# Tokens of the first feed-forward shared out, the first attention's tail reordered, and products that nobody reads added at waits of TensorE

## The chip, the cores and the metric

The kernel runs on one core of one Trainium2 chip, as one launch. The metric is the device time of that launch in microseconds. TensorE (PE in the profile) multiplies matrices, VectorE (DVE), ScalarE (ACT) and GpSimd (POOL) do the elementwise work, and SyncE (SP) issues all DMAs. The engines run side by side and wait for each other by semaphores only.

## The reference

The input x has 8 sequences of 256 tokens with 512 features, and a context of 8 x 256 x 128. Two layers follow, each an attention onto the context and a feed-forward, all with a layernorm before and a residual after:

```
x = x + L0_xattn(layernorm(x), ctx)     # 16 heads of 32, causal, softmax(q k / sqrt(32)) v, Wout
x = x + L0_ffn(layernorm(x))            # tokens rounded to 8 bits, weights to -1, 0, 1; silu between
x = x + L1_xattn(layernorm(x), ctx)     # 16 heads with latent keys of 64 (rope on the context)
x = x + L1_ffn(layernorm(x))            # 8 experts of width 16, the 2 best of each token
```

In L0_ffn a token row is divided by its own largest magnitude over 127 and rounded, multiplied by W1 (512 x 2048), and the hidden row is treated in the same way ahead of W2 (2048 x 512).

## The kernel before, in words

Everything is in tiles of 128 tokens. There are 16 tiles, two to a sequence, and X holds them all in SBUF with their means and variances (mv) and inverse deviations (rstd). The program is a row of blocks. In a block each engine has its own instruction list, and all engines meet before the next block begins. The blocks are: layer0_attention, layer0_feed_forward, score_weights (weight products of the second attention), the second attention itself (layer1_attention) and layer1_experts.

**Split products.** Where full precision is wanted, a matrix a is kept as a_h (ScalarE writes it, rounded) and a_l = a - a_h (VectorE or GpSimd), and `products` (L41) issues three products for each pair: low by high, high by low, high by high. A projection of the first attention (`project`, L396) is 12 such products for the queries and 3 for the keys.

**The first attention.** TensorE follows a list of steps written out by hand: BEGIN0, then FIRST0 for batch 0, STEPS0 for batches 1 to 7 and END0 (L185). For every group i of four heads there are: `S` the scores, `TY`, `TZ`, `TX` the transposes of the probabilities (keys 0 for heads 0 and 1, keys 0 for heads 2 and 3, keys 1), `pv` the product with the values, and `proj` the projection of the next batch. `lnt` transposes normalised tokens, `v` makes values, and `out` is the output projection of one tile of tokens: 12 products of 512 columns. Every step but S writes one of four PSUM banks in turn, and `take_bank` (L340) lets TensorE wait until the holder of four steps ago has been read. Around a group, VectorE finds the maxima (L757), ScalarE does the exponentials (L524), VectorE inverts the sums (L766), GpSimd multiplies the probabilities (`normalise`, L667). Then ScalarE copies the transposed keys 0 and VectorE keys 1 (`copy_probs`). After pv, ScalarE and VectorE split the result (`split_c`), and the two tiles of out need the split of all four groups.

Beside that, the weights W1 and W2 are brought to -1, 0, 1 in pieces at numbered positions of each batch (`weights_at`), on VectorE as one operation of 128 x 512 a piece (`quantise`, L834). Three of the pieces fall on positions 5, 6 and 7 of the last batch.

**The first two tiles of the feed-forward** are prepared in the attention's block. GpSimd normalises them in the last batch between groups 2 and 3 (`early_tokens`, L686). VectorE rounds them (`quantise_early_tokens`, L965): a maximum, four small operations and two passes of 512, with a drain after most. Tile 0 is transposed on TensorE (`xt`) and copied by ScalarE into early_xqT. Tile 1 is transposed in the feed-forward's block.

**The feed-forward** (`step`, L1041) is a loop over t from -2 to 15. At each t, TensorE transposes the rounded hidden row of tile t, multiplies tile t + 2 by W1 (`up`, 16 products of 512 columns), multiplies tile t by W2 (`down`, 16 products) and transposes the tokens of tile t + 3.

**The start.** Tiles 0 and 1 of x and the matrix Wq are the first loads. VectorE measures both tiles (L850 to L860), GpSimd makes the inverse deviations in six small operations (`pool_deviations`, L160), VectorE normalises both tiles (L867), and TensorE transposes both once the second is done (L386). ScalarE rounds the four quarters of Wq (L581) ahead of all else, and VectorE makes the four low parts (L871). The first projection waits for both transposed tiles, split, and for all four low parts.

## Time and profile before

| | us |
|---|---|
| median of 3 runs | 1033.93 |
| lowest and highest | 1032.07 to 1035.49 |
| the profiled execution's own time | 1032.81 |
| its span, from the first to the last instruction | 1030.8 |
| outside the span | 2.0 |

The profile is of one execution. Its blocks end at about 284.4 (first attention), 422.4 (feed-forward), 444.6 (weight products) and 981 us (second attention). Times in the rows are microseconds from the span's start. An x and a number after a tile's name says how many instructions of that kind the row merges, and its duration then runs from the first start to the last end. "idle before" in square brackets is how long the engine had stood still, with what it waited for. TensorE's clock has two levels, 1.2 and 2.4 GHz, shown as 0.50 and 1.00 of the granted clock.

### The profile page before, as it was taken

What the parts mean: (1) busy time and instruction counts of PE and PEld (TensorE: products, weight loads), DVE (VectorE), ACT (ScalarE), POOL (GpSimd) and SP (SyncE); (2) the same over time, 40 slices, a digit from 0 to 9 for tenths busy, and PEclk for the clock granted to TensorE, in tenths of its full rate; (3) what the DMA queues carried; (4) which work ended last, traced back from release to release, by engine and by line L of the source; (5) the groups of instructions that cost most, each with busy time, mean ns of one, the idle gap of its engine ahead of it and who ended that gap; (6) DMA issues with size and microseconds to landing.
All of it is one profiled execution on the core that took longest, in us unless ns stands there. A gap on an engine that the chain in (4) does not pass through costs nothing. (4 is left out here: it accounts for less than half of the span.)

```text
span 1030.8 us, 20634 instructions
## 1 busy us (share of the span) xinstructions
PE 972.3 (94%) x7756; PEld 761.5 (74%) x7772; DVE 754.6 (73%) x1646; ACT 631.0 (61%) x1691; POOL 319.8 (31%) x379
## 2 busy tenths in 40 slices
PE   5889999998789999889999999999999999999997
PEld 4677778786545555447888888888888888888796
DVE  5768998886678998266667767677676776767586
ACT  4578888786478787465555545555555555555462
POOL 5766777455534430520020020200202002000461
PEclk9899999998999999999999999999999999999998
DMA  8130121000093000530000000000000000000013
GB/s 288 39 142 2 48 89 43 2 2 2 2 255 133 1 1 1 183 104 1 1 22 1 1 22 1 22 1 1 22 1 22 1 1 1 1 2 1 1 43 123
DMA packets 20131, 41.92 MB, mean 41 GB/s; under 512 B 1216, under 2 KB 4544, under 8 KB 19520
## 3 DMA queue, kind: packets, MB, share of 16 engines
q1 hardware_dynamic: 20032, 40.59, 11.7%
q8 instruction: 63, 1.03, 0.4%
q14 instruction: 36, 0.29, 0.1%
HBM read 36.39 MB, written 4.19 MB: 39 GB/s over the span
## 5 line engine op out<-in xcount | busy, mean ns | idle before, releaser
L1577 ACT ACTIVATE c_h<-c_bank_b 128x512 fp32r<-128x512 f32 x64 | 38.3, 598 | 158.2 <-PE c_bank_b L1489 158.2
L673 POOL TENSOR_TENSOR a_probs<-a_probs,a_inv 128x256 f32<-128x256 f32 (+1 forms) x128 | 109.7, 884 | 65.6 <-DVE a_inv L774 65.1
L1591 ACT ACTIVATE probs<-c_score,c_neg_max 128x256 f32<-128x256 f32 x256 | 119.0, 480 | 9.8 <-DVE c_neg_max L1671 9.7
L533 ACT ACTIVATE a_probs<-a_s,a_neg_max 128x128 f32<-128x128 f32 (+1 forms) x256 | 104.2, 436 | 28.0 <-DVE a_neg_max L762 27.9
L1661 DVE TENSOR_TENSOR c_l<-c_bank_b,c_h 128x512 fp32r<-128x512 f32 x64 | 44.2, 691 | 103.7 <-ACT c_h L1577 103.7
L45 PE MATMUL c_acc<-VO_h,c_l 128*128 128x512 f32 x256 | 101.7, 397 | 1.4 <-DVE c_l L1661 1.4
L47 PE MATMUL c_acc<-VO_h,c_h 128*128 128x512 f32 x256 | 100.7, 393 | 0.0
L1582 ACT ACTIVATE c_pT_h<-c_turn 128x512 fp32r<-128x512 f32 x128 | 69.6, 597 | 50.3 <-PE c_turn L1479 50.3
L46 PE MATMUL c_acc<-VO_l,c_h 128*128 128x512 f32 x256 | 100.0, 391 | 0.0
L1310 POOL TENSOR_TENSOR c_ctx_raw<-c_ctx_raw,c_table 128x1024 f32<-128x1024 f32 x8 | 19.0, 2378 | 226.3 <-PE c_bank_b L1489 213.4
L1666 DVE TENSOR_TENSOR c_pT_l<-c_turn,c_pT_h 128x512 fp32r<-128x512 f32 x128 | 81.9, 681 | 1.4 <-ACT c_pT_h L1582 1.4
L1671 DVE TENSOR_REDUCE c_neg_max<-c_score 128x2 f32<-128x512 f32 x128 | 81.7, 680 | 0.8
L1679 DVE TENSOR_SCALAR probs<-probs,c_inv 128x256 f32<-128x256 f32 x256 | 75.6, 358 | 5.0
L45 PE MATMUL c_bank_a<-c_yT_h,A_l 128*128 128x256 f32 x256 | 77.1, 301 | 0.0
L162 POOL TENSOR_SCALAR c_var<-g_mean_var 128x2 f32<-128x2 f32 x7 | 1.6, 225 | 228.3 <-DVEq L1692 228.3
L47 PE MATMUL c_bank_a<-c_yT_h,A_h 128*128 128x256 f32 x256 | 72.4, 283 | 0.0
L46 PE MATMUL c_bank_a<-c_yT_l,A_h 128*128 128x256 f32 x256 | 71.9, 281 | 0.0
L1479 PE MATMUL c_turn<-g_ident,probs 128*128 128x128 f32 x512 | 69.5, 279 | 0.0
L762 DVE TENSOR_REDUCE a_neg_max<-a_s 128x2 f32<-128x256 f32 (+1 forms) x128 | 63.4, 548 | 2.7 <-PE a_s L381 2.3
L1657 DVE TENSOR_TENSOR c_qk_l<-c_bank_a,c_qk_h 128x512 fp32r<-128x512 f32 x64 | 44.0, 687 | 23.6 <-ACT c_qk_h L1573 23.6
L1479 PEld LDWEIGHTS c_turn<-g_ident,probs 128*128 128x128 f32 x512 | 55.1, 140 | 7.8 <-DVE probs L1679 0.3
L1069 PE MATMUL b_down<-w,b_hqT 128*128 128x512 bf16 x255 | 57.8, 379 | 1.6 <-ACT b_hqT L1086 1.5
(278 smaller groups left out, 2859.1 us busy)
## 6 DMA issues: line engine op xcount, KB each, us to landing
w_raw<-in_w SPq DMA_DIRECT2D x8, 1024.0 KB, 5.7
wq<-in_wq SPq DMA_DIRECT2D x1, 4096.0 KB, 23.0
c_ctx_raw<-in_ctx SPq DMA_DIRECT2D x8, 512.0 KB, 3.3
wo<-in_wo SPq DMA_DIRECT2D x1, 4096.0 KB, 14.9
out<-g_x SPq DMA_DIRECT2D x16, 256.0 KB, 2.1
g_x<-in_x SPq DMA_DIRECT2D x7, 512.0 KB, 6.5
wq_raw<-in_wq SPq DMA_DIRECT2D x4, 256.0 KB, 5.5
a_ctx_raw<-in_ctxT SPq DMA_DIRECT2D x8, 128.0 KB, 2.8
```

The lines of the kernel that those rows point to most:

```text
L45: pe.matmul(out, ll, rh, start=start and n == 0, stop=False)
L46: pe.matmul(out, lh, rl, start=False, stop=False)
L47: last = pe.matmul(out, lh, rh, start=False, stop=stop and n == len(pairs) - 1)
L533: last = act.activation(probs[i % 2][:, 2 * pair + j, at], s[:, 2 * pair + j, at], ACT.Exp, bias=neg_max[:, pair, q, j:j + 1], accum_out=s ...
L673: last = pool.tensor_tensor(p, p, inv[:, pair, q, :].unsqueeze(2).broadcast_to([P, 2, (q + 1) * P]), ALU.mult)
L762: last = dve.tensor_reduce(neg_max[:, pair, q, :], s[:, 2 * pair:2 * pair + 2, q * P:(2 * q + 1) * P], AX.X, ALU.max, negate=True)
L1479: last = pe.transpose(turn[k][:, hq * P:(hq + 1) * P], probs[p % 2][:, hq, k * P:(k + 1) * P], ident[:, :])
L1582: act.activation(pT_h[:, k, :], turn[k][:, :], ACT.Copy).then_inc(turn_hi, 1)
L1591: last = act.activation(probs[p % 2][:, i, :], score[h][:, t, :], ACT.Exp, bias=neg_max[:, i:i + 1], accum_out=sums[:, i:i + 1])
L1666: dve.tensor_tensor(pT_l[:, k, :], turn[k][:, :], f32(pT_h[:, k, :]), ALU.subtract).then_inc(turn_lo, 1)
L1671: dve.tensor_reduce(neg_max[:, 2 * h:2 * h + 2], score[h][:, :, :], AX.X, ALU.max, negate=True).then_inc(maxed, 1)
L1679: last = dve.tensor_scalar(probs[p % 2][:, i, :], probs[p % 2][:, i, :], inv[:, i:i + 1], None, ALU.mult)
```

## The change: what it does

1. **Start.** VectorE clears a small tile (`blank`) and TensorE then multiplies it 36 times (128 x 128 by 128 x 256, bf16) into a bank that nobody reads. VectorE takes over the small operations of the first inverse deviations; GpSimd keeps the power alone. TensorE transposes a tile as soon as that tile is normalised. GpSimd makes two of the four low parts of Wq, ahead of its copy of the identity.
2. **Last batch of the first attention.** The three pieces of W2 at positions 5, 6 and 7 move behind the rounding of both early tiles. VectorE goes straight from the maxima of group 3 to both copies of keys 0 of group 2 (ScalarE's before), the inversion and copy that follow, and the split of group 1. GpSimd no longer normalises the early tiles; VectorE does so inside quantise_early_tokens.
3. **END0.** A step "fill0" of 5 products of 512 columns comes first. It takes a bank, as every step does. Both early tiles are transposed (xt0, xt1) between out0 and out1, and ScalarE copies both.
4. **Feed-forward.** Tile 1 comes ready from the block before, so its transpose and copy go. Products that nobody reads are added: 9 of 512 columns ahead of tile 1's up products, and in the last tile 10 of 256 columns ahead of the wait for the rounded hidden row, 4 ahead of the down products, 16 behind them.
5. **Weight products.** 10 products of 512 columns follow TensorE's last transpose of this block.

The diff, cut to its core:

```diff
+def keep_awake(pe, out, left, right, n):
+
+    for _ in range(n):
+        pe.matmul(out, left, right, start=True, stop=True)
...
-END0 = ["pv2'", "T3'", "pv3'", "xt0", "out0'", "out1'"]
+END0 = ["fill0", "pv2'", "T3'", "pv3'", "out0'", "xt0", "xt1", "out1'"]
...
-                sp.wait_ge(wq_lo, DC)
+                sp.wait_ge(wq_lo, DC // 2)
+                sp.wait_ge(wq_lo_pool, DC // 2)
+                sp.wait_ge(y_turned, 1)
...
-                        pe.wait_ge(y0_ready, 1)
+                        pe.wait_ge(y0_ready, i + 1)
...
-                            pe.wait_ge(wq_lo, DC)
+                            pe.wait_ge(wq_lo, DC // 2)
+                            pe.wait_ge(wq_lo_pool, DC // 2)
...
+                def keep_busy(n):
+
+                    for _ in range(n):
+                        pe.matmul(s[:, 0, 0:S], blank[:, 0:P], blank[:, :], start=True, stop=True)
+
+                pe.wait_ge(blanked, 1)
+                keep_busy(36)
...
+                    elif kind == "fill":
+                        keep_awake(pe, out[:, :], identb[:, :], mask[:].rearrange("p q k -> p (q k)"), 5)
                     elif kind == "xt":
-                        turn_early_tokens(out)
+                        turn_early_tokens(i, out)
...
-                copy_probs(B - 1, 2)
                 split_c(B - 1, 2)
                 copy_probs(B - 1, 3)
                 split_c(B - 1, 3)
-                act.wait_ge(early_turned, 1)
-                act.activation(early_xqT.rearrange("p c t -> p (c t)"),
-                               work[bank_of["xt", 0, 0]][:, 0:D // 2].bitcast(BF16), ACT.Copy)
+                for i in range(TPB):
+                    act.wait_ge(early_turned, i + 1)
+                    act.activation(early_xqT[:, i].rearrange("p c t -> p (c t)"),
+                                   work[bank_of["xt", 0, i]][:, 0:D // 2].bitcast(BF16), ACT.Copy)
...
-                def early_tokens():
-                    pool.wait_ge(y_turned, TILES)
-                    for i in range(TPB):
-                        pool.tensor_scalar(y[:, i, :], X[:, i, :], mv[:, i, 0:1], rstd[:, i:i + 1], ALU.subtract, ALU.mult
-                                           ).then_inc(early_y_ready, 1)
...
-                deviations(0).then_inc(rstd0_ready, 1)
-                pool.wait_ge(y0_ready, 1)
+                pool.drain()
+                pool.wait_ge(first_var_ready, 1)
+                pool.tensor_tensor(rstd[:, 0:TPB], first_var[:, :], power[:, :], ALU.pow).then_inc(first_root_ready, 1)
                 pool.wait_ge(ident_in, DMA)
+                for c in range(DC // 2, DC):
+                    pool.wait_ge(wq_hi, c + 1)
+                    pool.tensor_tensor(wq_l[:, c, :], wq_raw[:, c, :], f32(wq_h[:, c, :]), ALU.subtract).then_inc(wq_lo_pool, 1)
...
-                    if b == B - 1:
-                        early_tokens()
...
+                def copy_first_keys(b, i, pair):
+                    dve.wait_ge(p_turned, 3 * (b * 4 + i) + pair + 1)
+                    dve.tensor_copy(pT[:, 2 * pair:2 * pair + 2, 0:S],
+                                    work[bank_of["TZ" if pair else "TY", b, i]][:, :].rearrange("p (h t) -> p h t", h=2)
+                                    ).then_inc(k0_copied, 1)
...
+                dve.memset(blank[:, :], 0.0).then_inc(blanked, 1)
                 first_statistics(0)
                 first_statistics(1)
-                measure(0)
-                dve.wait_ge(rstd0_ready, 1)
+                dve.drain()
+                for tile in range(TPB):
+                    dve.bn_aggr(mv[:, tile, :], first_stats[:, tile, :])
+                dve.drain()
+                first = slice(0, TPB)
+                dve.tensor_scalar(first_var[:, :], mv[:, first, 1], EPS, None, ALU.add).then_inc(first_var_ready, 1)
+                dve.wait_ge(first_root_ready, 1)
+                dve.tensor_tensor(first_sq[:, :], rstd[:, first], rstd[:, first], ALU.mult)
+                dve.drain()
+                dve.tensor_tensor(first_sq[:, :], first_sq[:, :], first_var[:, :], ALU.mult)
+                dve.drain()
+                dve.tensor_scalar(first_sq[:, :], first_sq[:, :], -0.5 * SCALE, 1.5 * SCALE, ALU.mult, ALU.add)
+                dve.drain()
+                dve.tensor_tensor(rstd[:, first], rstd[:, first], first_sq[:, :], ALU.mult)
+                dve.drain()
                 for i in range(TPB):
-                    last = dve.tensor_scalar(y[:, i, :], X[:, i, :], mv[:, i, 0:1], rstd[:, i:i + 1], ALU.subtract, ALU.mult)
-                last.then_inc(y0_ready, 1)
-                for c in range(DC):
+                    dve.tensor_scalar(y[:, i, :], X[:, i, :], mv[:, i, 0:1], rstd[:, i:i + 1], ALU.subtract, ALU.mult
+                                      ).then_inc(y0_ready, 1)
+                for c in range(DC // 2):
                     dve.wait_ge(wq_hi, c + 1)
                     dve.tensor_tensor(wq_l[:, c, :], wq_raw[:, c, :], f32(wq_h[:, c, :]), ALU.subtract).then_inc(wq_lo, 1)
                 split_y(0, 0)
...
-                    weights_at(b, 5)
+                    if b < B - 1:
+                        weights_at(b, 5)
                     if b == 0:
                         first_statistics(6)
                         measure(5)
                     split_proj(b + 1, 2)
                     copy_probs(b, 1)
-                    weights_at(b, 6)
+                    if b < B - 1:
+                        weights_at(b, 6)
 
                     maxima(b, 3, 0)
                     maxima(b, 3, 1)
+                    if b == B - 1:
+                        copy_first_keys(b, 2, 0)
+                        copy_first_keys(b, 2, 1)
+                        invert(b, 3, 0)
+                        copy_probs(b, 2)
+                        split_c(b, 1)
+                        break
...
-                    dve.wait_ge(early_y_ready, i + 1)
+                    dve.tensor_scalar(y[:, i, :], X[:, i, :], mv[:, i, 0:1], rstd[:, one], ALU.subtract, ALU.mult)
+                    dve.drain()
...
-                copy_probs(B - 1, 2)
+                dve.wait_ge(early_rstd_ready, 1)
+                dve.wait_ge(y_turned, TILES)
                 quantise_early_tokens(0)
                 split_c(B - 1, 2)
                 copy_probs(B - 1, 3)
                 split_c(B - 1, 3)
                 quantise_early_tokens(1)
+                for pos in (5, 6, 7):
+                    weights_at(B - 1, pos)
...
+                def awake(t, n):
+                    out = down[:, :] if t < 0 else xT[:].rearrange("p c t -> p (c t)").bitcast(F32)
+                    keep_awake(pe, out, identb[:, :], w1[:, 0, 0:D if t < 0 else S], n if t < 0 else 2 * n)
+
                 def step(t, par):
+                    if t == -1:
+                        awake(t, 9)
+                    if t == TILES - 1:
+                        awake(t, 5)
...
-                        tokens = xqT if t + 2 > 0 else early_xqT
-                        if t + 2 > 0:
-                            pe.wait_ge(x_copied, t + 2)
+                        tokens = xqT if t + 2 >= EARLY else early_xqT[:, t + 2]
+                        if t + 2 >= EARLY:
+                            pe.wait_ge(x_copied, t + 3 - EARLY)
...
+                    if t == TILES - 1:
+                        awake(t, 2)
...
-                    if has(t, 3):
-                        rounded = xq[1 - par] if t + 3 >= EARLY else early_xq[t + 3]
-                        after(pe, x_quant, t + 4 - EARLY)
-                        after(pe, x_copied, t + 2)
+                    if t + 3 >= EARLY and has(t, 3):
+                        pe.wait_ge(x_quant, t + 4 - EARLY)
+                        after(pe, x_copied, t + 3 - EARLY)
                         for c in range(DC):
-                            last = pe.transpose(xT[:, c, :], rounded[:, c * P:(c + 1) * P], identb[:, :])
+                            last = pe.transpose(xT[:, c, :], xq[1 - par][:, c * P:(c + 1) * P], identb[:, :])
                         last.then_inc(x_turned, 1)
                 all_steps(pe, step)
+                awake(TILES, 8)
...
+                keep_awake(pe, banks[0][:, :], identb[:, :], identb[:, :].unsqueeze(1).broadcast_to([P, 4, P]), 10)
```

## Rows read from the trace of the kernel before

**Rows 1.** The page: busy time by engine

```profile
PE 972.3 (94%) x7756; PEld 761.5 (74%) x7772; DVE 754.6 (73%) x1646; ACT 631.0 (61%) x1691; POOL 319.8 (31%) x379
```

**Rows 2.** Stretches: length; busy PE, PEld, DVE, ACT, POOL; clock, DMA

```profile
284.40:422.40 138.00, 128.32 (x812) 67.53 (x828) 113.91 (x216) 103.87 (x96) 41.80 (x21) 1.00 0.25 73
...
422.40:444.60 22.20, 18.83 (x168) 11.23 (x168) 6.40 (x9) 12.47 (x21) 13.79 (x13) 1.00 0.72 261
...
444.60:981.00 536.40, 531.03 (x3505) 442.47 (x3505) 375.95 (x799) 284.65 (x807) 64.17 (x79) 1.00 0.03 9
...
46.70:49.50 2.80, 2.48 (x29) 2.19 (x26) 2.79 (x6) 1.05 (x3) 2.28 (x5) 0.50 0.32 56
...
244.80:254.50 9.70, 8.65 (x70) 6.05 (x67) 4.21 (x9) 5.15 (x20) 4.16 (x5) 0.50 0.01 3
```

**Rows 3.** Order of time, TensorE after two waits (start, duration, idle before)

```profile
45.13 0.66 PE L425 MATMUL a_work<-g_ident,a_probs 128*128 128x128 f32 x4 [2.23 <-DVE a_c_l L788]
...
422.52 1.71 PE L1224 MATMUL cw_bank<-kcq,wqr 128*64 128x128 f32 x27 [2.13 <-PEq L1031]
```

**Rows 4.** Order of time, VectorE, ScalarE, GpSimd in the first 15 us

```profile
7.83 1.00 DVE L867 TENSOR_SCALAR y<-g_x,g_mean_var,g_rstd 128x512 f32<-128x512 f32 x2 [2.69 <-POOLq L173]
...
7.35 2.61 ACT L581 ACTIVATE wq_h<-wq_raw 128x512 fp32r<-128x512 f32 x4 [5.35 <-DMA wq_raw<-in_wq]
...
8.91 2.49 POOL L701 CAST g_identb<-g_ident 128x128 bf16<-128x128 f32 x1 [1.16 <-DVE y L867]
...
12.98 1.54 POOL L703 TENSOR_TENSOR wkv_l<-wkv_raw,wkv_h 128x512 fp32r<-128x512 f32 x1 [1.59 <-ACT wkv_h L588]
```

**Rows 5.** Order of time, TensorE, the first projections

```profile
12.50 0.58 PE L45 MATMUL a_work<-a_yT_h,wq_l 128*128 128x256 f32 x1 [1.57 <-DVE a_yT_l L746]
...
15.81 0.28 PE L45 MATMUL a_work<-a_yT_h,wq_l 128*128 128x256 f32 x1
...
17.61 0.33 PE L376 MATMUL a_s<-a_qk_h,a_qk_l 32*128 32x128 f32 x4
```

**Rows 6.** Order of time, VectorE, last batch of the first attention

```profile
263.40 1.01 DVE L838 SCALAR_TENSOR_TENSOR w<-w_raw,a_limit,w 128x512 bf16<-128x512 f32 x1
...
264.94 0.92 DVE L838 SCALAR_TENSOR_TENSOR w<-w_raw,a_limit,w 128x512 bf16<-128x512 f32 x1
...
265.79 1.94 DVE L762 TENSOR_REDUCE a_neg_max<-a_s 128x2 f32<-128x256 f32 x4
...
277.52 0.68 DVE L968 TENSOR_REDUCE a_early_amax<-y 128x1 f32<-128x512 f32 x1
...
279.76 0.43 DVE L977 TENSOR_SCALAR early_xq<-early_yr 128x512 bf16<-128x512 f32 x1
...
283.61 0.69 DVE L802 TENSOR_TENSOR g_x<-g_x,a_work 128x512 f32<-128x512 f32 x1 [2.11 <-PE a_work L47]
```

**Rows 7.** Order of time, GpSimd and ScalarE, last batch

```profile
265.31 4.57 POOL L689 TENSOR_SCALAR y<-g_x,g_mean_var,g_rstd 128x512 f32<-128x512 f32 x2
...
269.85 3.17 POOL L673 TENSOR_TENSOR a_probs<-a_probs,a_inv 128x256 f32<-128x256 f32 x4
...
270.27 1.13 ACT L544 ACTIVATE a_pT<-a_work 128x512 f32<-128x512 f32 x2
```

**Rows 8.** Order of time, TensorE, last batch and the feed-forward's tile 1

```profile
271.55 0.96 PE L441 MATMUL a_work<-a_pT,V 128*32 128x256 f32 x8 [4.59 <-ACT a_pT L544]
...
277.75 0.47 PE L45 MATMUL a_work<-wo_h,a_c_l 128*128 128x512 f32 x1 [0.72 <-DVE a_c_l L788]
...
289.93 3.63 PE L1060 MATMUL b_up<-w,b_xqT 128*128 128x512 bf16 x16 [1.47 <-ACT b_xqT L1101]
```

**Rows 9.** Order of time, TensorE, into the second attention

```profile
444.81 0.63 PE L1445 MATMUL c_bank_a<-g_ident,c_y 128*128 128x128 f32 x4 [3.23 <-PEq L1204]
...
445.71 3.52 PE L1511 MATMUL c_acc<-wo,kckv 128*128 128x512 f32 x4
...
452.62 1.88 PE L1511 MATMUL c_acc<-wo,kckv 128*128 128x512 f32 x4
```

More of the change, by code:

```diff
@@ L199, in steps_of_layer0 @@
                 own = b + (1 if kind in ("proj", "v") or "~" in x else 0) + (2 if "+" in x else 0) - (1 if "'" in x else 0)
-                if kind == "xt":
+                if kind in ("xt", "fill"):
                     own = 0
@@ L487, in _ @@
                         add_sums(i, out)
+                    elif kind == "fill":
+                        keep_awake(pe, out[:, :], identb[:, :], mask[:].rearrange("p q k -> p (q k)"), 5)
                     elif kind == "xt":
-                        turn_early_tokens(out)
+                        turn_early_tokens(i, out)
                     else:
@@ L1098, in step @@
                                            ).then_inc(silued, 1)
-                    if has(t, 3):
-                        act.wait_ge(x_turned, t + 3)
+                    if t + 3 >= EARLY and has(t, 3):
+                        act.wait_ge(x_turned, t + 4 - EARLY)
                         act.activation(xqT[:], xT[:], ACT.Copy).then_inc(x_copied, 1)
@@ L1289, in _, with layer1_attention @@
                 dve.tensor_tensor(kr_l[:, :], kr[:, :], f32(kr_h[:, :]), ALU.subtract)
[L1292 removed]
+def layer1_attention(nc, io, X, mv, rstd, ident, identb, store, ahead, ahead_in, expert_raw, expert_in, first):
     with Memory(nc, "c") as m:
@@ L2003, in program @@
         ahead_in = g.sem("ahead_in")
-        early = ([store.place(f"early_xq{i}", 3, [P, 3, D], BF16)[:, i, :] for i in range(TPB)],
-                 store.place("early_xqT", 3, [P, 3, DC, P], BF16)[:, 2, :, :], g.sb("early_s1", [P, TPB]))
+        early = ([store.place(f"early_xq{i}", 3, [P, 4, D], BF16)[:, i, :] for i in range(TPB)],
+                 store.place("early_xqT", 3, [P, 4, DC, P], BF16)[:, 2:4], g.sb("early_s1", [P, TPB]))
         expert_raw = (g.sb("wd", [P, DC, G + E]), g.sb("wu", [P, D]), g.sb("iota", [P, E]))
```

29 lines of the change are left out of this document (17 added, 12 removed).

## The prediction, made before the changed kernel was run

> **What bounds the kernel now.** I read the page first: TensorE is busy for 94% of the span, and the next engine for 73% [rows 1]. Then the stretches. The second attention keeps TensorE busy for 531 of 536 us, so whatever comes before it moves the end one for one [rows 2]. In single stretches the granted clock is 0.50, which is the lower level of 1.2 GHz: 2.8 us at 46.7, and 9.7 us at 244.8 although TensorE was busy for 8.65 of them [rows 2]. Then the waits ahead of them, in order of time. The fall at 46.7 came 1.6 us after TensorE had stood still for 2.23 us. Another stop of 2.13 us, ahead of 422.52, was followed by no fall: the block that begins there has a clock of 1.00 [rows 2, 3]. So a stop of about 2 us may cost the clock or not. All parts of the change lie ahead of the second attention, in places where TensorE waits.
>
> **Start.** GpSimd's six small operations hold VectorE for 2.69 us ahead of the first normalised tile. ScalarE is busy with Wq from 7.35 to 9.96, and only then can it take a transposed tile [rows 4]. So the inverse deviations and the earlier transposes gain almost nothing. The first projection starts at 12.50, released by the last split tile. The split was late because VectorE first made four low parts; now it makes two, and the tiles should be split at about 11.9. But the two parts on GpSimd are a new wait. The third quarter of Wq is rounded at 9.3, and one such part costs between 1.14 and 1.54 us: 1.54 is the row of the same operation at 12.98, and 1.14 is that row less the 0.4 us in which VectorE held it. They end between 11.6 and 12.7; I take 12.1 [rows 4, 5]. What queues behind them on GpSimd is the identity copy and the values' low part, which ended at 14.5 and may now end at up to 15; both are used only from the first scores on, at 17.61 [rows 5].
>
> The row of the identity copy shows what could go wrong: 128 columns took 2.49 us, as long as VectorE's four low parts beside it [rows 4]. The Trainium skill says the same (SBUF — State Buffer, "Who interferes with whom"): a VectorE instruction with two SBUF inputs and a GpSimd instruction that reads SBUF exclude each other. By that rule GpSimd's third quarter starts only at about 9.5, when VectorE's second is done, and the trace agrees. The split of the tiles reads a bank and only one SBUF input, so by the rule it leaves GpSimd alone; if it blocked it too, the projection would start at about 13.4.
>
> The clock is the larger term. The first 15 products of the projection take 3.31 us, the next 15 take 1.80 with what follows [rows 5]: the clock was at its lower level until 15.7, which the granted clock of the profile does not show. With it up the start would gain 1.5 us. The 36 products of 256 columns run at 0.22 each from about 1.1 us: to 9.0 if all are slow, to about 7 if the clock rises on the way. Transposes follow to about 9, then TensorE waits 3 us until the projection. Stops of 2.23 us were followed by a fall, so I expect the clock to be down again for most of the projection. Bounds: 1.9 us gained (high clock, start at 12.1), 0.9 lost (start at 13.4, low clock). I take 0.3 gained, near the lower row of the clock.
>
> **Last batch.** VectorE's two pieces ahead of the maxima take 1.01 and 0.92 us, and the maxima start at 265.79 [rows 6]. Without the pieces they start at 264.0. ScalarE's exponentials follow at the same distance and end 1.8 us earlier: 268.5, where its copy starts at 270.27 now. GpSimd's early tiles (4.57 us) sit ahead of its last probabilities, which start at 269.85 and end at 273.0 [rows 7]. With the tiles gone, they wait only for VectorE's inversions at 267.3 and 268.8, and end at about 270.6.
>
> TensorE stands still for 4.59 us until ScalarE has copied keys 0 of group 2, at 271.55 [rows 8]. Now VectorE copies them: two operations of 512 columns at 0.69 [rows 6], after the maxima, so until 267.2; keys 1 until 267.9, the split of group 1 until 268.3. The fill step takes the bank of group 1's pv. It therefore waits for that split, though nobody reads its products, and pv of group 2, whose data are ready at 267.9, is queued behind it. Five products of 512 columns at 0.22 (3.63 us for 16 [rows 8]) hold it until 269.4. That is hidden: the transposes of group 3 behind it need GpSimd's 270.6. They end at 272. At the low clock the fill costs 2.2 and is no longer hidden.
>
> The next in line is VectorE. It rounds tile 0 from 268.8: 2.67 us as for tile 1 (277.52 to 280.19 [rows 6]) and 0.50 for the normalisation [rows 4], to 272.1. Then come the split of group 2, keys 1 of group 3 (0.69), pv, the split of group 3: the output projection can start at 274.6 against 277.75 [rows 8], 3.1 us earlier. Its 24 products take what they take now. Between the halves there are now two transposes instead of none, 0.3 us each, and the second needs tile 1, rounded at 274.5 + 3.2 = 277.7; the first half ends at 277.4. So the second half ends at about 280.95. The three moved pieces (3 x 0.7) and the first addition fit under it, to 280.6. The last addition ends at 281.75 where it ended at 284.30 [rows 6]: 2.55 us. Bounds: the output projection's whole 3.1, and 1.0 if the clock falls among these steps. I take 2.5.
>
> **Feed-forward.** Tile 1's up products start at 289.93, released by the copy that now goes [rows 8]. The nine products ahead of them take 9 x 0.22 = 2.0, and after tile 0's up products they end at a time that matches 290.2 of now, 0.3 later than today. ScalarE reaches tile 1's silu only at 294.1, so that is hidden. At the end TensorE waits 2.13 us for the block to close, until 422.52 [rows 3]. The 16 products (16 x 0.11 = 1.8) fit in, with little to spare: nothing to 0.1 lost. The 14 others lie in waits longer than themselves. The clock of this block is 1.00 now [rows 2], so there is nothing to win either: 0 in all, between -0.3 and 0.3.
>
> **Weight products.** TensorE stands still for 3.23 us ahead of 444.81. The next four products take 3.52 us, and four of the same shape later take 1.88 [rows 9]: the low clock again. The ten products end at about 443.7, before VectorE has closed the block, so they cost nothing, and leave a stop of 1.1 us, half of the shortest one that preceded a fall in rows 3. Three heads of two such rows each run before the projection: they take 3.9 us and would take 2.6. I take 1.3; between 0 (it falls all the same) and 1.7.
>
> **Sum.** 0.3 + 2.5 + 0 + 1.3 = 4.1 us against the profiled execution's own 1032.81, so 1028.7. That execution was 1.1 below the median of the runs, 1033.93, and for the median I say 1029.8. Three runs spread over 3.4 us, and about 0.3% (3.1 us) is what a measurement of this kernel can tell from no change.
>
> **The rivals.** (A) The clock stays up through the first projection: TensorE was at work for 8 us before the stop, where at 46.7 it had been waiting on and off. That adds 1.5: 1028.3. Against it stands the 3 us stop.
>
> (B) The clock falls in the tail. Between 268 and 274.6 TensorE has only the fill, transposes and narrow products, with gaps. In its favour: at 244.8 it was 89% busy with such work and stayed at 0.50 for 9.7 us [rows 2]. The transposes and pv of groups 2 and 3 then take 1.5 us longer and the tail gives back 1.0 instead of 2.5: 1031.3. The Trainium skill (TensorE: Matmul & The Clock Gate, Part 4) has a rule of that kind: transposes do not count as work in the same way. Rows 2 bear it out in part.
>
> (C) The added products do not hold the clock, and the change does not do what it says: only the reordering counts, 1033.93 - 2.5 = 1031.4. Against it: under the steady products of the second attention the clock reads 1.00 [rows 2].
>
> (D) Slower. If the clock is down when the output projection begins and stays down as long as at 244.8, its 24 products and tile 0's 16 up products run at twice their time. The fill costs 1.1 more and the transposes 1.5, which delays the projection by 2.6; the 24 add 5.6, the 16 add 3.5. Less the 2.5 and 1.3 won that is 8.9 slower: 1042.8. It decides from a low clock at 274.6 that lasts past 280.
>
> **How the numbers follow.** Forecast 52%, with a range of its own of 1028.3 to 1031.3; A 17%, B 18%, C 8%, D 5%. Faster by over 0.3% is a time below 1030.8: three quarters of the forecast case (0.39), nearly all of A (0.16), a quarter of B and of C (0.06), 0.61 in all. Slower by over 0.3% is D, 0.05. The rest, 0.34, is no change. The range reaches from below A to above B and C: 1026.8 to 1032.8.
>
> **What would show it.** The block after the first attention begins near 281.9 less the start's gain. TensorE's stop ahead of pv of group 2 shrinks from 4.59 to about 2. The clock row shows no 0.50 at 445, and the first four value products take 1.9. The first 15 projection products take 3.3 (forecast) or 1.7 (A). It would be wrong if GpSimd's low parts end after 13, if the fill of 5 holds back the transposes of group 3, if VectorE reaches the last addition after TensorE's last product, or if new falls of the clock appear in the first 70 us, where the shift moves every stop.

## The result: 1023.8 us where 1029.8 was forecast

The changed kernel takes 1023.76 us (median of 6 runs, 1022.92 to 1027.26). The kernel before takes 1034.41 in the same comparison (6 runs). The ratio is 0.9913, with a 95% interval of 0.9894 to 0.9932. The change is faster by 7 to 11 us; the forecast was 4.1, and the time lies below the range of 1026.8 to 1032.8. A second set of 6 executions gave 1024.91, ratio 0.9937 [0.9913, 0.9962].

The profiled execution of the changed kernel took 1023.56 us, its span is 1021.7. The page of the changed kernel, busy time by engine; [rows 1] are the same of before:

```profile
PE 977.4 (96%) x7844; PEld 765.8 (75%) x7862; DVE 755.4 (74%) x1654; ACT 630.7 (62%) x1689; POOL 314.7 (31%) x374
```

TensorE is busy for 5 us more in a span that is 9 us shorter. The stretches of the changed kernel, first the same times as [rows 2] where the clock was down, then the stages (length; busy PE, PEld, DVE, ACT, POOL; clock, DMA):

```profile
46.70:49.50 2.80, 2.32 (x27) 1.48 (x25) 2.80 (x7) 2.29 (x8) 1.74 (x6) 1.00 0.49 170
57.00:63.60 6.60, 5.47 (x34) 4.33 (x35) 1.46 (x4) 4.18 (x19) 3.04 (x2) 0.50 0.27 108
244.80:254.50 9.70, 8.17 (x123) 6.42 (x124) 7.13 (x15) 8.11 (x25) 6.99 (x8) 1.00 0.01 3
278.90:416.60 137.70, 133.09 (x847) 70.97 (x862) 113.47 (x216) 103.19 (x95) 41.55 (x21) 1.00 0.25 73
416.60:438.90 22.30, 21.01 (x179) 12.20 (x179) 6.40 (x9) 12.48 (x21) 13.77 (x13) 1.00 0.73 260
438.90:1012.00 573.10, 567.58 (x3794) 477.77 (x3794) 408.27 (x932) 305.93 (x865) 84.13 (x98) 1.00 0.04 13
1012.00:1021.70 9.70, 3.55 (x14) 2.38 (x14) 5.02 (x13) 0.63 (x2) 0.62 (x1) 1.00 0.43 162
```

The line to look at is the third. No part of the change touches the work at 244.8, yet the 9.7 us that ran at 0.50 before have a clock of 1.00, and the row counts 123 products there instead of 70. (The low stretch of before lasts 10.2 us in all; the window leaves out its edges.) The same holds for the last line. This is the kernel before at its end:

```profile
1012.00:1022.00 10.00, 8.12 (x56) 7.15 (x55) 8.28 (x36) 2.89 (x12) 1.25 (x2) 1.00 0.29 107
1022.00:1030.80 8.80, 4.67 (x13) 2.82 (x11) 3.17 (x5) 0.38 (x1) 0.62 (x1) 0.54 0.33 121
```

Its last 8 us are at the lower level. So two stretches that the forecast took as given are gone, and so is the one at 46.7. At 57.0 the changed kernel is low for 6.6 us, where before was low for 3.4 at 60.

The start in the changed kernel (order of time, TensorE and GpSimd), against [rows 4, 5]:

```profile
1.04 6.40 PE L488 MATMUL a_s<-blank 128*128 128x256 bf16 x36 [1.04 <-DVE blank L889]
9.22 2.50 POOL L723 TENSOR_TENSOR wq_l<-wq_raw,wq_h 128x512 fp32r<-128x512 f32 x2 [3.10 <-ACT wq_h L604]
11.86 0.36 PE L45 MATMUL a_work<-a_yT_h,wq_l 128*128 128x256 f32 x1 [2.98 <-POOL wq_l L723]
...
15.86 0.36 PE L45 MATMUL a_work<-a_yT_h,wq_l 128*128 128x256 f32 x1
...
17.09 0.33 PE L389 MATMUL a_s<-a_qk_h,a_qk_l 32*128 32x128 f32 x4
```

The last batch in the changed kernel, VectorE and TensorE, against [rows 6 to 8]; the scores of the last group start at 259.03 here and at 262.25 before:

```profile
260.76 1.95 DVE L783 TENSOR_REDUCE a_neg_max<-a_s 128x2 f32<-128x256 f32 x4
262.62 1.28 DVE L789 COPY a_pT<-a_work 128x512 f32<-128x512 f32 x2
...
265.21 1.03 PE L54 MATMUL a_work<-a_mask,g_identb 128*128 128x512 bf16 x4 [2.12 <-DVE a_c_l L815]
266.17 0.64 PE L455 MATMUL a_work<-a_pT,V 128*32 128x256 f32 x8
...
268.39 0.43 DVE L1028 TENSOR_SCALAR early_xq<-early_yr 128x512 bf16<-128x512 f32 x1
...
271.29 0.47 PE L45 MATMUL a_work<-wo_h,a_c_l 128*128 128x512 f32 x1 [1.05 <-DVE a_c_l L815]
...
277.69 0.69 DVE L829 TENSOR_TENSOR g_x<-g_x,a_work 128x512 f32<-128x512 f32 x1 [1.10 <-PE a_work L47]
```

The two later places in the changed kernel, TensorE, against [rows 3, 9]:

```profile
414.30 1.91 PE L54 MATMUL b_xT<-w,g_identb 128*128 128x256 bf16 x16
416.60 3.60 PE L1288 MATMUL cw_bank<-kcq,wqr 128*64 128x128 f32 x62 [0.39 <-PEq L1085]
...
435.48 2.32 PE L54 MATMUL cw_bank<-g_identb 128*128 128x512 bf16 x10
438.87 0.63 PE L1510 MATMUL c_bank_a<-g_ident,c_y 128*128 128x128 f32 x4 [1.08 <-PEq L1268]
439.77 1.88 PE L1576 MATMUL c_acc<-wo,kckv 128*128 128x512 f32 x4
```

### The profile page after: what moved, and what is told of

It reads as the page before. It is cut to its first block and busy times, and to the rows that moved or that the text cites. A ratio compares the mean times of both kernels' runs of the same rounds, so it can differ in the third digit from the quotient of the medians.

```text
span 1021.7 us, 20814 instructions
## 1 busy us (share of the span) xinstructions
PE 977.4 (96%) x7844; PEld 765.8 (75%) x7862; DVE 755.4 (74%) x1654; ACT 630.7 (62%) x1689; POOL 314.7 (31%) x374
```

## The experiments

Some words first: a stop is a time in which TensorE stands still, a fall is a change of its clock to the lower level, and low time is the time spent at that level. Two measures serve for all experiments. The first is the mean granted clock c of an execution. The lower level is half of the upper, so 2 x (1 - c) of the span was spent low: for the profiled kernel before, 2 x 0.017 x 1030.8 = 35 us, and the low stretches of its trace add up to 35.5 (36, 46, 60, 244, 271, 445 and 1022 us). The start needs care. The clock is on record only from 15.3 to 17.9 us on in the profiles with the old start, and from 4.3 to 6.6 us on in those with the new one; ahead of that it counts as 1.00. The kernel before runs its first projection at the lower level until 15.7, by the durations, and this is not counted; with the new start it is: 3.4 us in the two profiles of the changed kernel, 6.8 in that of the start alone. The second is the length of seven stages between fixed points of TensorE's work in each profile. The times by kernel, over the executions of the 15 runs below, of the kernel before beside them, and of the changed kernel's first comparison, where equal kernels are put together. The 15 runs were made in four comparisons on four chips; the mean of the kernel before lies between 1032.4 and 1033.6 us in them, so differences of these means can be off by about 1 us. Three of the 94 executions of the kernel before are left out: one of 2530 us, and two of 1036.1 and 1036.6 us whose mean clock is 0.941, where all others have 0.980 or more:

```
kernel                                  executions  mean us  mean low us
before                                          91  1032.96         33.9
before + start alone                             5  1030.09         32.1
before + reordered tail, no added products      12  1033.10         36.9
before + 10 products behind weight products     18  1030.13         24.7
before + 4 products in batch 6                   5  1031.01         27.6
before + 5 products in batch 7's stop           12  1031.08         27.0
before + 8 products at 671 us                   12  1034.12         27.8
changed                                         12  1024.71         18.5
changed - products of tail and feed-forward      9  1026.64         23.8
changed - start                                  8  1027.02         21.9
changed - 10 products                           11  1027.60         25.3
changed - 10 products + 12 at the end            8  1027.87         25.8
changed + products in five stops, misplaced      6  1026.29         12.7
changed + products in five stops, mended         6  1022.88          9.3
```

A fit over these 215 executions, with one constant for each kernel and one slope for all, gives 0.35 us (+-0.026) of time for 1 us of low clock; what is left scatters by 0.8 us. The constants take up what the start leaves uncounted. It would be 0.5 if TensorE set the pace in all of them. The fit rests on leaving out the two executions at 0.941: they have some 120 us of low time and are only 3 to 4 us slower than the mean, and with them the slope would be 0.11. Why they are so fast is not known.

**Start alone.** From the changed kernel: the 36 products, the statistics on VectorE, half of the low parts on GpSimd.

```diff
+                pe.wait_ge(blanked, 1)
+                keep_busy(36)
...
+                for c in range(DC // 2, DC):
...
-                for c in range(DC):
...
+                for c in range(DC // 2):
```

> The kernel before with part 1 of the change alone (the start). In the pair of profiles the first scores came 0.5 us earlier (17.61 to 17.09). Theory P (the instants at which the clock is set are not the program's, so a shift of the program decides which stops of TensorE cost the clock): 0.5 us gained directly, and the stretch of 9.7 us at the low clock in batch 7 comes or goes from run to run; runs then lie in two groups some 4 us apart, so the median is 1029 to 1034. Theory W (the 36 products at the start are what later keeps the clock up in batch 7): the stretch is gone in every run, 1029.5.

Measured: 1029.98, ratio 0.9956 [0.9943, 0.9969]: some 3 us instead of 0.3. Theory W is out: the profile has a low stretch of 6.8 us in batch 7. That profile is of the slowest of the five executions (1032.30) and shows next to nothing of the gain; its first scores start at 18.72, later than before's 17.61. In the table the low time is only 1.8 us less than before's, but 3.4 to 6.8 us of it are the first projection, which is not counted for before. Elsewhere it is thus 5 to 9 us less, 1.8 to 3.0 us of time by the fit.

**Reordered tail alone.** With the shared first tokens, without start and added products.

```diff
-END0 = ["pv2'", "T3'", "pv3'", "xt0", "out0'", "out1'"]
+END0 = ["pv2'", "T3'", "pv3'", "out0'", "xt0", "xt1", "out1'"]
```

> The kernel before with the reordered tail and the shared tokens alone: no start, and none of the products that nobody reads. Both theories: 2.7 us gained if the clock holds in the tail, some 1.2 less if it falls there. Batch 7 up to group 2 is as before, so under P and W alike most runs keep the stretch at the low clock: 1031 to 1033. If the tail's order itself is what removed the stretch, 1027.

Measured: 1033.54, ratio 0.9994 [0.9981, 1.0007]. In its profile the tail, from the last group's scores to the feed-forward's first product, is 19.37 us (22.59 before): gained as forecast, and a little more. But the feed-forward takes 140.9 instead of 137.7, and the median lies above the 1031 to 1033 that were expected. The trace has two falls in the feed-forward:

```profile
294.00:297.40 3.40, 3.02 (x20) 2.20 (x21) 2.73 (x3) 3.30 (x4) 2.27 (x1) 0.51 1.08 266
416.00:419.40 3.40, 2.65 (x7) 1.04 (x8) 1.23 (x3) 1.52 (x2) 0.00 (x0) 0.64 0.00 0
```

**Ten products behind the weight products alone**, run twice in different comparisons.

```diff
                 for n in range(DC, 2 * DC):
                     turn_weight(n)
+                keep_awake(pe, banks[0][:, :], identb[:, :], identb[:, :].unsqueeze(1).broadcast_to([P, 4, P]), 10)
```

> The kernel before with the 10 products behind the weight products alone. 1.7 us gained ahead of the second attention's first scores (7.63 less 5.94 in the pair of profiles), nothing elsewhere: 1032.3 to 1032.7 by both theories. If the clock falls all the same, 0.

> The kernel before with the 10 products behind the weight products alone, once more, since this edit of one place gained 4.9 us where 1.3 were forecast. Theory P (it takes the stretch at 445 us away, and with it most of the end's low-clock time): no stretch at 439 to 449 us, at most 3.6 us of low clock behind 1017 us, median 1028 to 1030. Rival Q (the first time was luck): the end's stretch is 6 us or longer and the median 1031 to 1032.5.

Measured: 1028.45, ratio 0.9955 [0.9937, 0.9972], and then 1030.62, ratio 0.998 [0.9962, 0.9998]. Over the 18 executions the mean is 2.8 us below that of the kernel before, twice the forecast. The first time was partly luck: its profile had no low stretch in batch 7, 200 us ahead of the edit. The second time the end's stretch was down to 1 us, as theory P had it, but the median lies between the two theories.

**A small delay ahead of the stop in batch 7.** Four products of 512 columns in front of the scores of batch 6's first group, and nothing else.

```diff
+                    if slot == 24:
+                        for _ in range(4):
+                            pe.matmul(s[:, 0, :], identb[:, :], mask[:].rearrange("p q k -> p (q k)"), start=True, stop=True)
```

> The kernel before with 4 products of 512 columns that nobody reads, ahead of the scores of batch 6, group 0, where TensorE is busy anyway: a shift of about 0.9 us of all that follows, as batch 7 of the changed kernel is 0.8 later than before. Theory P: the stretch at the low clock in batch 7 goes in most runs or changes its length, and the kernel is about 3 us faster although it has more to do: 1030 to 1032. Theory W, or a cause in the changed parts themselves: 0.9 slower, 1035.

Measured: 1030.68, ratio 0.9967 [0.9954, 0.9979]. Pure extra work made the kernel faster. TensorE's stop in batch 7 is as long as before, and the clock behind it stays up. First the kernel before, TensorE at the stop and at the dense output products behind it, which run at the lower level:

```profile
244.48 0.48 PE L376 MATMUL a_s<-a_qk_h,a_qk_l 32*128 32x128 f32 x4 [2.35 <-ACT a_probs L533]
...
249.00 0.77 PE L45 MATMUL a_work<-wo_h,a_c_l 128*128 128x512 f32 x1 [1.05 <-DVE a_c_l L788]
```

Then the kernel with the delay, TensorE, and its stretch:

```profile
247.66 0.33 PE L379 MATMUL a_s<-a_qk_h,a_qk_l 32*128 32x128 f32 x4 [2.36 <-ACT a_probs L536]
```

```profile
247.60:257.30 9.70, 8.58 (x125) 6.75 (x126) 7.51 (x16) 7.70 (x23) 6.58 (x7) 1.00 0.01 3
```

The profile alone would not show the cause, since the first one with the 10 products lacks this stretch too, without any edit ahead of it. The five executions do: the ratio is below 1, and their low time is 6.3 us less than before's.

**Holding the clock in that stop.**

```diff
+                    if slot in (29,):
+                        pe.wait_ge(exped, 2 * slot - 1)
+                        for _ in range(5):
+                            pe.matmul(s[:, 0, :], identb[:, :], mask[:].rearrange("p q k -> p (q k)"), start=True, stop=True)
```

> The kernel before with 5 products of 512 columns issued in the stop ahead of the scores of batch 7's second group, with nothing else changed. Theory P (the gain of the change that was not forecast is a low-clock stretch of 9.7 us in batch 7, which begins in this stop): the clock stays at 1.00 over 244 to 255 us, scores of the third group start 3.5 to 4.0 us earlier, median 3 to 4 us below the kernel before. Rival Q (which stretches are low follows the time since the start, and a product here or there does not alter it): the stretch stays or comes somewhere else within 20 us, median within 1 us of before.

Measured: 1031.46, ratio 0.9986 [0.9972, 1.0]. The stretch is gone, and batch 7 from its second to its third group takes 7.33 us instead of 11.38. But stretches of 3.4 us stand at 267 and 291 us, behind it, and the mean gain is 1.9 us; 3 to 4 were expected.

**The changed kernel less one part each.** Without the products of tail and feed-forward (fill0 and the three calls of awake):

> The changed kernel without its added products in the tail, in the feed-forward stage and behind it; it keeps the new start, the reordered tail and the 10 products behind the weight products. Theory P (the added products keep the clock up, and without them the feed-forward stage has the falls at 294 and 416 us that the reordered tail alone showed, 3.2 us): median 1026 to 1028, feed-forward stage 139 to 141 us long. Rival Q (these products are worth nothing, as the prediction held for the stage itself): 1023.0 to 1024.5, stage 137.7 us.

Measured: 1026.72, ratio to before 0.9943 [0.9923, 0.9962]. Its feed-forward is 140.6 us, with low stretches at 289 and 412. Without the new start:

> The changed kernel with the start of the kernel before: no 36 products on a zeroed tile, statistics and low parts as before. Theory P (the start is worth its own 0.5 us and also shifts what follows; the start alone gave 3.4 us by median): 1025 to 1028. Rival Q (the start is worth only the 0.5 us by which the first scores came earlier): 1024.0 to 1024.6.

Measured: 1027.74, ratio 0.9942 [0.992, 0.9963]. Its profile has the 10.2 us in batch 7 again. Without the 10 products:

> The changed kernel without the 10 products behind the weight products. Theory P and the prediction's step agree on the place: a low-clock stretch of 3.4 us at the second attention's start (about 439 us) in most executions, weight products to first score 1.3 to 1.7 us longer, median 1.0 to 1.7 us above the changed kernel. Rival Q (the 10 products' gain was an accident of one profile, since the kernel before with them alone gained 4.5 us, three times this): no stretch there and the median the same within 0.5 us, or 3 to 4.5 us above it.

Measured: 1027.15, ratio 0.9951 [0.9935, 0.9967]. That is 2.2 us above the changed kernel in the same comparison, more than the 1.0 to 1.7 of theory P. The stretch at 441 is there, and one more, at the very end (the changed kernel without the 10 products):

```profile
441.00:444.40 3.40, 3.40 (x10) 1.85 (x9) 1.43 (x3) 1.79 (x3) 0.00 (x0) 0.53 0.58 169
1018.00:1027.00 9.00, 4.64 (x12) 2.73 (x10) 3.17 (x5) 0.38 (x1) 0.34 (x1) 0.50 0.31 117
```

**Each kernel once more, unaltered.**

> The changed kernel, unaltered, once more. Theory P (which stops cost the clock differs from execution to execution of one and the same program; what the change did is to leave fewer and shorter stops at which it can): the profile has low-clock stretches at places and lengths that are not all those of the first one (12, 36, 57, 1022 us), the mean clocks of the runs spread by 0.003 or more, the median is 1022.5 to 1025. Rival Q (the stretches belong to the program): the same four stretches within 1 us, clocks 0.992 to 0.993 in nearly all.

> The kernel before, unaltered, profiled once more. Theory P: the stretch of 10.2 us in batch 7 and those at 271, 445 and 1022 us are partly absent, or others stand beside them; the sum of the low stretches after the start is 25 to 39 us. Rival Q: the same seven stretches (36, 46, 60, 244, 271, 445, 1022 us) within 1 us and with the same lengths.

Measured: 1024.91 for the changed one; 1034.1 for the kernel before, ratio to itself 1.0017 [0.9997, 1.0038]. Of the second profile of the kernel before, the stretches that differ from the first:

```profile
57.00:63.80 6.80, 4.67 (x31) 3.53 (x32) 2.41 (x5) 3.37 (x15) 4.05 (x2) 0.57 0.44 181
244.80:254.50 9.70, 7.69 (x80) 5.68 (x80) 5.87 (x14) 7.14 (x26) 5.59 (x8) 0.82 0.01 3
416.00:419.40 3.40, 3.38 (x9) 1.25 (x10) 0.60 (x2) 0.80 (x1) 0.00 (x0) 0.55 0.00 0
1022.00:1030.00 8.00, 3.54 (x14) 2.38 (x14) 3.81 (x9) 0.38 (x1) 0.62 (x1) 1.00 0.44 166
```

One program, and in one execution the clock falls at 416 and not at the end, in the other the reverse. The stretch in batch 7 is 3.4 us instead of 10.2. The clocks of the changed kernel spread from 0.987 to 0.993, those of before from 0.981 to 0.992. Rival Q is out for both.

**A delay in mid-kernel, and the end filled.** These two ask why 10 products at 436 us should matter at 1018.

> The kernel before with 8 products of 512 columns, 1.9 us, ahead of an output product of the second attention's batch 3 (some 650 us, where TensorE has no stop), so that all behind comes later with respect to the stretch at 445 us, which stays. If the length of the end's stretch hangs on when the last stop comes, counted from the stretch at 445 us: the end has under 5 us of low clock where the kernel before had 8.3, and the median is 0 to 1 us above before. If it does not (holding the clock at 445 us is what counts): 6 to 11 us at the end, median 1.5 to 2.2 us above before.

> The changed kernel without the 10 products behind the weight products, and with 12 products in the experts' stop of 1.9 us near 1014 us. If the end's long stretch (11.1 us in the changed kernel without the 10 products) comes from this stop: at most 2 us of low clock behind 1017 us, span behind the first score of the second attention 1.5 to 2.5 us shorter than 575.9, median 1025 to 1026. If it comes whatever this stop holds: a stretch of 6 us or more stays, median 1027 to 1028.

The edits, the first in the second attention's output product (`project_out`) of the kernel before, the second in the experts (`expert_out`) of the changed kernel without the 10:

```diff
+                    if b == 3 and p == 0:
+                        keep_awake(pe, acc[0][:, :], VO_h[:, 0, 0:P], VO_h[:, 0, :], 8)
...
+                    if b == B - 2:
+                        keep_awake(pe, hidden[0][:, 0, :], wd_h[:, 0, 0:P], wd_h[:, 0, :], 12)
```

Measured: 1034.5, ratio 1.0014 [0.9995, 1.0033], for the delay, and 1027.28, ratio 0.9953 [0.9934, 0.9972], for the end filled. With the delay the fall at 446 is still there and the end is clean (the kernel before with 8 products, which came at 671 us):

```profile
446.00:449.40 3.40, 3.40 (x12) 1.86 (x12) 1.43 (x3) 1.68 (x3) 0.00 (x0) 0.63 0.76 211
1022.00:1031.90 9.90, 3.91 (x17) 2.51 (x15) 5.56 (x14) 1.02 (x4) 0.62 (x1) 1.00 0.42 159
```

From the second attention's first score to the end it takes 575.54 us, as before (575.51), although 1.9 us of products were put in. Over its 12 executions the low time is 6 us less than before's. So the clock need not be held at 445 for the end's stretch to go; the second profile of the kernel before says the same. That the fall at the end depends on when the last stop comes fits this, but is not shown: the mean clock does not say where the 6 us were saved. Filling the stop itself took the end's stretch away too, but a new fall at 466 used up the gain in that profile, and the median did not move. That half of the expectation was missed.

**More stops filled.** The first try had two of its sets in wrong places: 14 products behind a wait, so that the first projection started 1.8 us late, and 12 ahead of the wrong tile.

> The changed kernel with more products of the same kind in five further stops: 14 ahead of the first projection, 5 ahead of the scores of batch 0's third group, 12 ahead of the turning of batch 2's first tile, 5 ahead of the scores of batch 7's second group, 12 in the experts' stop of 1.9 us. Theory P (each low-clock stretch that is left costs half its length): the stretches at 12, 36 and 57 us (13.6 us together) go, first scores at 15.4 us instead of 17.1, median 1018 to 1020. Rival Q (added products take the place of work or the clock falls at another stop): median 1022 to 1025.

> The changed kernel with products that nobody reads in five more stops, now so that none stands between a result that is there and its reader: 18 ahead of the first projection's wait, 3 ahead of the scores of batch 0's third group, 12 ahead of the turning of batch 3's first tile (the stop of 3.0 us at 55.1), 5 ahead of the scores of batch 7's second group, 12 in the experts' stop of 1.9 us. Theory P (each 3.4 us of low clock avoided gives 1.2 to 1.7 us): stretches at 12 and 57 us gone, median 1018.5 to 1021.5. Rival Q (a stop filled moves the fall to the next stop): median 1023 to 1025 with as much low clock as in the changed kernel.

Measured: 1025.99, ratio 0.9935 [0.9912, 0.9959], and mended 1022.88, ratio 0.9914 [0.9892, 0.9937]. Both lie above what theory P gave (1018 to 1020, and 1018.5 to 1021.5). The mended version ran from 1021.76 to 1023.88 where the changed kernel, in the same comparison, ran from 1023.85 to 1028.25: it beats both kernels, by some 2 us over the changed one. Its first projection, the mended version:

```profile
8.71 2.13 PE L54 MATMUL a_work<-blank 128*128 128x256 bf16 x18
11.82 0.36 PE L45 MATMUL a_work<-a_yT_h,wq_l 128*128 128x256 f32 x1 [0.97 <-POOL wq_l L730]
15.57 0.33 PE L392 MATMUL a_s<-a_qk_h,a_qk_l 32*128 32x128 f32 x4
```

With a stop of 0.97 us the clock stays up and the first scores start at 15.57, 1.5 us earlier. By batch 0's third group the lead is gone (34.73 against 34.59). Its mean low time is 9.2 us less than the changed kernel's, its mean time only 1.8 us less.

## Why the prediction was wrong

The step that failed is the one behind the sum 0.3 + 2.5 + 0 + 1.3: beside the start it priced one fall of the clock, at 445 us, and kept all the others of the one trace as they were. The difference of the means is 1032.96 - 1024.71 = 8.2 us. By the fit, 15.4 us less of low clock are 5.4 us, and 2.8 are left for everything else. Without the 3.4 us at the first projection, which are counted in the changed kernel alone, it is 18.8 us less, 6.7 us of time, and 1.6 are left. Either way the clock was worth four to five times the 1.3 that the forecast had for it, and everything else no more than the 2.8 forecast (0.3 + 2.5). This is a split by a fit, not a measurement of each part; the stages show where the time went.

By stages, as means over the profiles with and without the part that bears on each stage:

```
stage                                          without   with  gained  forecast
start to first scores                            18.10  17.57     0.5       0.3
first scores to batch 7's second group          227.41 228.06    -0.7       0
batch 7, second to third group                   10.44   7.77     2.7       0
last scores to feed-forward                      22.55  19.79     2.8       2.5
feed-forward                                    138.35 137.68     0.7       0
weight products to the attention's first score   32.75  31.05     1.7       1.3
first score of the second attention to the end  575.22 573.90     1.3       0
```

(Profiles in each: rows 1 to 3, 7 without the new start and 6 with it, those with a delay or products in batches 6 and 7 or further ones in the start left out; row 4, 8 and 9; row 5, 8 kernels with the old tail and 7 with the new one and its products; row 6, 9 and 8; row 7, 7 and 8.) They add up to 9.0, which is near the 8.2 of the means. The four stages for which the forecast had a term (start, tail, feed-forward, weight products) gained 5.7 us of it, and the three that it took as given 3.3.

**Start: place right, and missed what it does further on.** GpSimd's second low part released the projection at 11.86 (forecast 12.1); two took 2.50, so 1.25 each, inside 1.14 to 1.54. VectorE's split of the tiles, from 10.27 to 11.56, ran beside them without holding them, so the feared start at 13.4 did not come. The clock was up for the first 6 products and down until 15.86: the first 15 took 2.7 us, between the forecast case (3.3) and rival A (1.7). The gain of 0.5 us is small against the spread of the profiles (17.4 to 18.5 without, 17.0 to 18.7 with the new start), and it was lost again by batch 7. But with the new start only 1 of 6 profiles had a low stretch behind batch 7's stop, against 6 of 7 without it, and such a stretch makes the stage up to 4 us longer. That fits the 2 to 3 us by which the start alone, and the changed kernel less the start, differ from their neighbours; the one profile of the start alone is the exception. The prediction did name new falls in the first 70 us as what would make it wrong; the changed kernel's one at 57.0 is longer than before's, but 5 of the 7 profiles with the old start have 6.8 us there too, so none is shown to be new.

**Tail: right step by step.** Counted from the scores of the last group: maxima at +1.73 (forecast +1.75), keys 0 copied by +4.87 (+4.95), pv of group 2 at +7.14 (+7.15), tile 0 rounded by +9.79 (+9.85), output projection at +12.26 (+12.35), last addition over by +19.35 (+19.50). Rival B did not come: the clock stayed up through fill, transposes and narrow products, and in all 9 profiles with the new tail this stage takes between 19.4 and 19.9 us, so nothing of the 1.5 us that B would have given back. The fill was not needed for that: the two profiles without fill0 (reordered tail alone, and without the products of tail and feed-forward) take 19.4 and 19.9 us as well. One thing the prediction did not see: all 8 profiles with the old tail are low for 3.4 us in this stage (6.8 in one), at 271.7 in the kernel before, right behind the stop of 4.59, and none of the 9 with the new tail is. So part of the 2.8 us is a fall that went with its stop; how much is not measured apart. And its argument for B misread the stretch at 244.8: more than half of it, from 249.00 on, was twelve dense output products of 128 x 512, not transposes and narrow products with gaps. The rule of the Trainium skill that stood behind B, that transposes do not count as work in the same way (TensorE: Matmul & The Clock Gate, Part 4), does not show in this stretch.

**Feed-forward: the step that said "The clock of this block is 1.00 now [rows 2], so there is nothing to win either: 0 in all" failed.** It took the one execution for the program. Of the 8 profiles with the old tail 3 have a feed-forward of 139.2 to 139.4 us; with the new tail and no added products both have 140.6 and 140.9; with the products all 7 have 137.68. So the products are worth 0.7 us against the old tail, and 3.1 against the new tail without them. That is why the reordered tail alone gained nothing.

**Weight products: the term that was mis-sized.** "I take 1.3" for this place: it is 1.7, in 17 profiles without exception (32.70 to 32.77 without, 31.05 to 31.07 with), the upper bound. The stop left was 1.08 us (forecast 1.1). Not forecast are the 1.3 at the end of the kernel: that stage is 573.6 to 574.1 us in all 8 profiles with the 10 products, and 575.0 to 576.0 in 6 of the 7 without. Together that is 3.0, as the removal (2.9) and the single runs (2.8) say.

In rival D there is a slip of 1.0 us: 2.6 + 5.6 + 3.5 - 2.5 - 1.3 is 7.9 and not 8.9, so its time would be 1041.8. D did not come, and nothing else hangs on it.

Behind the misses stands the one step named above: edits were costed against the falls of one trace. Two delays that only add work (4 products in batch 6, 8 products at 671 us) have the next fall missing in their profiles and 6 us less of low time over their executions, and a repeat of the same program moved falls as well. So which stops cost the clock does not follow from the length of the stop, and work put in elsewhere changes it. That much is shown. What remains open is why the new start sets batch 7 right more often than not (5 of 6 profiles against 1 of 7, few as they are), and why the fall at the end follows the 10 products so regularly: that it hangs on when the stops come fits both, but no run shows it.

## What to carry to other kernels

Before costing anything, read the clock row of several executions and turn the mean clocks into time at the lower level: here there were 34 us of it, by the fit some 12 us of the kernel (an estimate, since no run is free of it), and one trace said little about where they go. A reordering that saves 2.7 us but leaves other stops may give it all back in the next dense stage; products that nobody reads, in waits longer than themselves and ahead of no wait that matters, kept it. Where stops of some 2 us abound, forecast the change in the number of stops at risk, not only the fall beside the edit, and widen the range by the spread between executions.

## What was not expected of the hardware

- A stop of 2.35 us ahead of batch 7's second group was followed by 10.2 us at 0.50 in one kernel, and one of 2.36 us by none in another, with the same work on both sides; and 4 extra products 36 us earlier made the whole kernel 1.9 us faster by the means.
- The clock, once down in batch 7, stayed at 0.50 for 10.2 us, although TensorE was 89% busy in the 9.7 us of the row, more than half of them with dense products; in the second attention it came back after 3.4 us in each of the nine profiles that have a fall at its start.
- 1 us at the lower level cost 0.35 us on average: 0.5 in the weight products' stage (1.7 for 3.4), and little at the start, where the 1.5 us that the mended version won up to the first scores were lost within 20 us.
- GpSimd's cast of 128 columns, 2.49 us in [rows 4], takes 0.49 in the changed kernel, where it comes at 11.66 and VectorE's low parts are over:

```profile
11.66 0.49 POOL L724 CAST g_identb<-g_ident 128x128 bf16<-128x128 f32 x1
```
